# First attention of a two-layer decoder: each value product of 512 queries as two halves of 256 at neighbouring places of TensorE's order

## The reference, cut to what matters

```python
q, k, v = split(layernorm(x) @ w_qkv, 3)           # 16 heads of width 8
q1, q2 = split(q, 2); k1, k2 = split(k, 2)          # two half-heads of width 4
a1 = softmax(q1 k1^T / sqrt(8)); a2 = softmax(q2 k2^T / sqrt(8))   # 512 x 512
out = (a1 - lam * a2) @ v                           # then RMS norm per head, @ wo
```

## Time and profile before

| | |
|---|---|
| three runs | 1028.32, 1030.67, 1035.21 us; median 1030.67 |
| profiled execution | span 1028.4 us; the page gives no other time for it |
| TensorE busy (modelled ends) | 925.0 us, 90% |
| VectorE busy | 761.6 us, 74% |
| ScalarE busy | 624.5 us, 61% |
| GpSimd busy | 510.8 us, 50% |
| first value product to last | 42.9 to 393.4 us |

### The profile page before, as it was taken

How to read it: one execution, slowest core, us unless ns; L and a number is a source line. 1 busy time by engine, 2 the same in 40 slices (tenths; PEclk the granted TensorE clock), 3 DMA queues, 4 the chain that set the end, 5 groups by cost and what they waited for, 6 DMA issues and landing times. The chain is left out here.

```text
span 1028.4 us, 20270 instructions
## 1 busy us (share of the span) xinstructions
PE 925.0 (90%) x6146; PEld 480.8 (47%) x6146; DVE 761.6 (74%) x1656; ACT 624.5 (61%) x1500; POOL 510.8 (50%) x847
## 2 busy tenths in 40 slices
PE   3999999999999997899889999999999997888296
PEld 1222222222332334565455555555555564567296
DVE  7799899889999976889745666666656665676464
ACT  4388888888888883233266665665566652354164
POOL 6366666776554462100144454455445443775544
PEclk8599999999999999999999999999999997696599
DMA  4099920000000000000060000000000000000240
GB/s 103 1 237 245 245 60 1 2 1 2 2 1 0 0 1 1 1 1 1 8 206 6 15 9 7 8 13 5 8 5 13 0 2 1 0 2 16 89 122 19
DMA packets 50684, 37.49 MB, mean 36 GB/s; under 512 B 15737, under 2 KB 48677, under 8 KB 50608
## 3 DMA queue, kind: packets, MB, share of 16 engines
q1 hardware_dynamic: 48864, 32.83, 13.4%
q0 software_dynamic: 1744, 3.72, 1.1%
HBM read 15.54 MB, written 21.45 MB: 36 GB/s over the span
## 5 line engine op out<-in xcount | busy, mean ns | idle before, releaser
L725 DVE TENSOR_REDUCE a_nmax<-a_rows 128x2 f32<-128x1024 f32 x256 | 299.7, 1218 | 26.5 <-PE a_rows L439 23.6
L979 ACT ACTIVATE a_probs<-a_turned 128x512 f32<-128x512 f32 x512 | 270.0, 605 | 48.2 <-PE a_turned L465 46.9
L1451 POOL TENSOR_TENSOR a_prob<-a_prob,a_rinv 128x256 f32<-128x256 f32 (+3 forms) x128 | 159.4, 1253 | 163.9 <-DVE a_rinv L1647 163.6
L1640 DVE TENSOR_REDUCE a_nmax<-a_score 128x2 f32<-128x256 f32 (+3 forms) x128 | 105.6, 825 | 116.5 <-PE a_score L1497 112.2
L1594 ACT ACTIVATE a_prob<-a_score,a_nmax 128x128 f32<-128x128 f32 (+3 forms) x256 | 132.6, 523 | 81.9 <-DVE a_nmax L1640 81.3
L465 PE MATMUL a_turned<-a_q,a_qk 32*128 32x512 bf16 x512 | 136.9, 389 | 7.3 <-ACT a_probs L979 4.9
L424 PE MATMUL a_acc<-a_probs,a_vg 128*32 128x512 f32 x1024 | 138.1, 611 | 0.2
L439 PE MATMUL a_rows<-a_qk 32*128 32x512 bf16 x512 | 108.9, 398 | 5.9 <-DVE a_nmax L725 3.9
L465 PEld LDWEIGHTS a_turned<-a_q,a_qk 32*128 32x128 bf16 x512 | 34.9, 91 | 153.8 <-ACT a_probs L979 125.8
L1494 PE MATMUL a_score<-a_k_s,a_q_s 64*128 64x384 f32 (+3 forms) x512 | 103.7, 481 | 2.2 <-ACT a_prob L1594 1.3
L1653 DVE COPY a_pt<-a_turn 128x128 f32<-128x128 f32 (+3 forms) x224 | 92.2, 447 | 1.4 <-PE a_turn L1508 1.4
(11 more groups left out here) (351 smaller groups left out, 1580.7 us busy)
## 6 DMA issues: line engine op xcount, KB each, us to landing
xs_sorted<-a_blank SPq DMA_DIRECT2D x9, 1935.0 KB
m_m_w<-L_ffn_w SPq DMA_DIRECT2D x8, 512.0 KB, 9.2
c_xs<-xs_sorted SPq DMA_DIRECT2D x23, 129.0 KB, 2.1
g_a_wq<-L_attn_Wq SPq DMA_DIRECT2D x32, 64.0 KB, 2.1
g_X<-x SPq DMA_DIRECT2D x4, 256.0 KB, 4.7
a_wgu<-L_ffn_gate_up_proj SPq DMA_DIRECT2D x1, 1024.0 KB, 5.5
a_wdn<-L_ffn_down_proj SPq DMA_DIRECT2D x1, 512.0 KB, 6.8
g_a_wk<-L_attn_Wk SPq DMA_DIRECT2D x8, 64.0 KB, 1.9
```

Of the source, the lines that this page charges most:

```text
L725: dve.tensor_reduce(nmax[i % 2][:, p // 2, (p % 2) * 2:(p % 2) * 2 + 2], rows[n % 2][:, :, :], AX_X, ALU.max, negate=True).then_inc(row_ou ...
L979: act.activation(probs[:, (tb % 2) * 4 + j, :], turned[n % 3][:, :], ACT.Exp, scale=float(HD0) ** -0.5).then_inc(turn_out, 1)
L1451: pool.tensor_tensor(pr, pr, spread(rinv[:, t % RING, :], 2, width), ALU.mult).then_inc(scl, 1)
L1640: dve.tensor_reduce(nmax[:, t % RING, :], score[t % 2][:, :, 0:width], AX_X, ALU.max, negate=True).then_inc(mx, 1)
```

## The change

`pv_group` becomes `pv_half`. Half 0 has the group's waits and multiplies queries 0 to 255, half 1 has no wait of its own and multiplies queries 256 to 511; only half 1 counts up `pv`. Half 0 stands at the group's place k, half 1 at k + 1, so at least one `turn_tile` comes between them. Half 0 of group 0 of an even unit clears the bank's accumulation flags. In odd bodies group 2 stood at k = 15; its halves now stand at 14 and 15, so its first half comes ahead of the pair `next` 4. Products, operands and sums are otherwise the same.

```diff
-            def pv_group(i, r, tb):
-                pe.wait_ge(turn_out, turn_item(i + 1, ("exp", 4 * tb + 3)) + 1 + TURNS0 * r)
...
-                for j in range(4):
-                    last = pe.matmul(acc[32 * j:32 * j + 32, :], vg[i % 2][:, tb, j // 2, :],
-                                     probs[:, (tb % 2) * 4 + j, :], start=(tb == 0 and i % 2 == 0),
-                                     stop=(tb == SB - 1 and i % 2 == 1))
-                last.then_inc(pv, 1)
+            def pv_half(i, r, tb, half):
+                if half == 0:
+                    pe.wait_ge(turn_out, turn_item(i + 1, ("exp", 4 * tb + 3)) + 1 + TURNS0 * r)
...
+                cols = slice(half * S // 2, (half + 1) * S // 2)
                 for j in range(4):
+                    last = pe.matmul(acc[32 * j:32 * j + 32, cols], vg[i % 2][:, tb, j // 2, :],
+                                     probs[:, (tb % 2) * 4 + j, cols], start=(half == 0 and tb == 0 and i % 2 == 0),
+                                     stop=(half == 1 and tb == SB - 1 and i % 2 == 1), skip_group_check=True)
+                if half:
+                    last.then_inc(pv, 1)
...
-                    if k == 3 and has_last(i):
-                        pv_group(i - 2, r, SB - 1)
-                    if k == 6 and has_turn(i):
-                        pv_group(i - 1, r, 0)
+                    if k in (3, 4) and has_last(i):
+                        pv_half(i - 2, r, SB - 1, k - 3)
+                    if k in (6, 7) and has_turn(i):
+                        pv_half(i - 1, r, 0, k - 6)
...
-                    if k == (11, 10)[i % 2] and has_turn(i):
-                        pv_group(i - 1, r, 1)
+                    if k in (11 - i % 2, 12 - i % 2) and has_turn(i):
+                        pv_half(i - 1, r, 1, k - (11 - i % 2))
...
-                    if k == (14, 15)[i % 2] and has_turn(i):
-                        pv_group(i - 1, r, 2)
+                    if k in (14, 15) and has_turn(i):
+                        pv_half(i - 1, r, 2, k - 14)
```

More of the change, by code:

```diff
@@ L413, in _ @@
         def _(pe):
-            def pv_group(i, r, tb):
-                pe.wait_ge(turn_out, turn_item(i + 1, ("exp", 4 * tb + 3)) + 1 + TURNS0 * r)
[L417 to L422, removed]
-                for j in range(4):
-                    last = pe.matmul(acc[32 * j:32 * j + 32, :], vg[i % 2][:, tb, j // 2, :],
-                                     probs[:, (tb % 2) * 4 + j, :], start=(tb == 0 and i % 2 == 0),
-                                     stop=(tb == SB - 1 and i % 2 == 1))
-                last.then_inc(pv, 1)
+            def pv_half(i, r, tb, half):
+                if half == 0:
+                    pe.wait_ge(turn_out, turn_item(i + 1, ("exp", 4 * tb + 3)) + 1 + TURNS0 * r)
+                    if tb == 0:
+                        if i == 0:
+                            lp.ready(pe, 2)
+                        if i % 2 == 0:
+                            wait(pe, os_, i // 2 + SIX // 2 * r)
+                        pe.wait_ge(vgs, i + 1 + SIX * r)
+                cols = slice(half * S // 2, (half + 1) * S // 2)
+                for j in range(4):
+                    last = pe.matmul(acc[32 * j:32 * j + 32, cols], vg[i % 2][:, tb, j // 2, :],
[3 more added lines that the diff above has]
+                    last.then_inc(pv, 1)
             def row_pair(at, what, i, r):
```

## The result

The changed kernel takes 1051.26 us (median of four runs, 1049.08 to 1060.31), the kernel before 1030.49 (four runs, 1028.32 to 1035.21): a ratio of 1.0216, 95% interval 1.0166 to 1.0265. It is 21 us slower, where 14.4 were forecast; 1045 was predicted and the range, 1022 to 1066, holds it.

The account below looks back on a forecast made before the run. TensorE sets the pace, with VectorE close behind. A slip of 0.90 us per two bodies x 16 = 14.4 us, on 1028.4 gives 1042.8; with the profiled span 2.3 under the median, 1045 us, range 1022 to 1066.

Parts of the forecast that it names:

- Half 0.57: On TensorE, a half was taken to last 0.57 us from its first pass to the next tile.
- lead: On TensorE, 0.31 us pass from the score tile between the halves to the first pass of half 1.
- 0.14: On TensorE, two halves take 1.14 us where a group took 1.00: 0.14 us more per group.
- The walk: One odd and one even body of the first attention followed in order with fixed lags; slip 0.90 us per two bodies.
- lag of 0.71: Time after which the count of a half reaches ScalarE, 0.71 us; a whole group's took 1.13.
- Tile to its exponent 0.42.: Lag from a score tile on TensorE to its exponent on ScalarE, taken as 0.42 us.
- Group 0 starts at 329.47.: In the odd body, TensorE's group 0 was to start at 329.47 us instead of 329.30.
- The sign asked of ScalarE: If the forecast is right, ScalarE's waits behind group 0 shrink.
- ScalarE is fed: Rival: earlier tiles keep exponents in a row, saving 15 of VectorE's 23.6 us idle time, 1016 us; chance 0.12.
- No difference: Rival: a half is half a group, the 0.31 falls into buffer waits, 1032 to 1038 us; chance 0.19.
- Nothing hides: Rival, much slower: up to 3.0 us lost per two bodies, 1079 us; chance 0.11.
- That choice: Bodies with a later projection were taken to slip as much as those without, 0.90 us per two bodies.

Follow-up runs that it names:

- E1: Against the kernel before: both halves of every group directly behind each other at the group's old place; 1031.73 us, ratio 0.9985.
- E10: Changed kernel, all four groups split, plus a third block of exponents so no exponent waits for a count; 1049.69 us (one run).
- E7: Against the kernel before: only group 3 split, in even bodies alone; 1037.64 us (one run), two bodies 21.18 us.
- E12: Changed kernel, but group 3 of odd bodies has its halves directly behind each other at k = 3; 1046.03 us, ratio 1.0114.
- E5: Against the kernel before: only group 0 split, at k = 6 and 7; 1028.18 us (one profiled run), two bodies 21.00 us.
- E11: The kernel with group 0 alone split, timed over ten runs against the kernel before; 1031.04 us, ratio 0.9963.

## Why the prediction was right, and where its size was off

**The mechanism held.** Half 0.57 (0.57 taken), lead 0.32 (0.31), copy of the accumulator 1.60 us behind the group's start (329.08 - 327.49 = 1.59 walked). E1 and E10 show the cause: with nothing between the halves all of the slip goes, though the passes are as many, and with no exponent held by a count 1.19 of 1.36 stays. E1 also corrects the reading of one term: I charged 0.14 to the half; it belongs to the second change of shape. The sum is the same.

**The walk was too short.** It gave 0.90 us for two bodies; they slipped by 1.36. (By its own lag of 0.71, exponent 12 of the even body would start at 344.11 + 0.71 = 344.82, not 344.89, and the walk would end at 0.83.) Starts in us behind the first pass of group 3 in the odd body, 327.49 in the walk and 341.06 after:

| | walk | after | behind the walk |
|---|---|---|---|
| group 0 | 1.98 | 2.25 | 0.27 |
| tile 7 | 2.73 | 2.82 | 0.09 |
| group 1 | 5.03 | 5.17 | 0.14 |
| the shift's transposes | 7.58 | 7.82 | 0.24 |
| group 3, even body | 10.94 | 11.29 | 0.35 |
| group 1, even body | 15.74 | 16.21 | 0.47 |

Two terms failed.

*"Tile to its exponent 0.42."* The first exponent of each block has one more wait before it, for a count (`k % 4 == 0` in the code shown ahead), and starts 0.50 behind its tile: 350.89 to 351.39, 355.81 to 356.31. So it was before: the exponent at 344.19 stands 0.50 behind its tile:

```profile
343.69 0.38 PE L465 MATMUL a_turned<-a_q,a_qk 32*128 32x512 bf16 x1
```

The walk took 0.42 for all, and three such exponents release the buffer that TensorE waits for next: 12 in the odd body (348.23, 0.53 behind its tile at 347.70) ahead of the shift's transposes, 0 ahead of group 3, and 8 ahead of group 1 (the wait of 0.41 at 356.96). At these three places the trace falls 0.10, 0.10 and 0.09 further behind the walk. That the added wait makes the difference of 0.08 is read from these rows and was not tried.

*"Group 0 starts at 329.47."* It started 0.27 later. Group 0 of an even unit begins a new sum in `acc` and waits until ScalarE has copied the old one out (`os_`). Before, that wait was all but filled: the copy ended at 328.63 + 0.60 = 329.23 and the group started at 329.30. I moved the copy by 0.45 us and did not ask who else waits for it. But only 0.09 of the 0.27 went on: the walk already had tile 7, behind half 0, wait until 330.22 for its buffer. So the 0.45 and 0.44 us that E7 and E12 put on this one split are not what the walk missed. By its lags, without this split tile 7 would have started at 329.30 + 0.57 = 329.87, so it had charged 0.35 by then (an estimate).

The other 0.09 or so came in small steps, whose cause stays open.

**Waits.** By the walk VectorE would be idle over 10 us more; it is 18.4 (44.9 - 26.5). The sign asked of ScalarE did not come: before, no wait stood behind group 0 of the even body (eight exponents in a row from 339.59); after, there is one, 0.29 at 356.31. So the rival "ScalarE is fed" has nothing for it here, and what the prediction held against it came true: the early exponents 4 and 12 wait for half 1. "No difference" falls: the 0.31 did not vanish into waits. "Nothing hides" falls too: by the terms, eight splits cost 8 x 0.45 = 3.6 us gross, of which waits filled 2.2.

**The same slip with later projections.** Two bodies, one with such a projection, went from 21.86 to 23.13 us in most places: +1.27 against 1.36 without. That choice was good, though not everywhere: the last two of the fourteen bodies in the first stretch slipped by 0.31 (23.09 to 23.40), and its mean is 7.86 / 7 = 1.12.

**From bodies to the sum.** The last value product starts at 411.06 instead of 393.40: 17.7 us of the 20.1 by which the span grew. The other 2.4 lie behind the first attention, where nothing was changed; E1, which costs nothing, has 2.0 there (span 1030.4, last value product 393.39), so they are not the split's. Against 14.4 the first attention was 3.3 short. That it was not 16 x 0.46 = 7.4 short is in part luck: beside the smaller slip just named, the clock rose sooner in the profiled run after (granted 0.76 over 45 to 50 us, 0.50 before), and the next copy of queries and keys stood at 53.27 us, before at 54.82.

## What to carry to other kernels

Products that were cut in two cost nothing here as long as they stayed side by side; what cost was an instruction of another tile shape between them, 0.46 us of TensorE's time for a group (1.46 against 1.00). Before interleaving two shapes on the engine that sets the pace, count the changes of shape per turn of the loop. Read a lag for each kind of instruction that uses it: one that waits for one thing more was 0.08 us later here, and three of them on the path of two bodies made over half of what the walk missed. And where a step finishes later, list all who wait for it, also those whose wait is all but filled at present.

## What the runs showed of the hardware

The granted clock of TensorE moved single runs by several us. The first bodies run at the lower level (0.50), and when it rises differs from run to run, also of the same kernel: over 45 to 50 us it was 0.61 in the run of E5 and 0.50 in that of E11. Stretches of the kernel before, then of the profiled run of E12 (columns as in the earlier trace rows):

```profile
40.00:55.00 15.00, 14.23 (x77) 3.28 (x75) 10.55 (x11) 9.02 (x18) 9.30 (x20) 0.64 0.07 18
55.00:66.00 11.00, 9.94 (x80) 2.88 (x77) 9.67 (x9) 9.29 (x19) 6.23 (x18) 1.00 1.05 284
66.00:77.00 11.00, 10.82 (x83) 3.15 (x82) 10.59 (x12) 9.64 (x20) 6.44 (x19) 1.00 1.10 245
```

```profile
55.00:66.00 11.00, 10.74 (x67) 2.85 (x64) 6.32 (x7) 6.30 (x12) 4.14 (x12) 0.50 1.08 283
66.00:77.00 11.00, 11.00 (x74) 3.16 (x76) 5.63 (x6) 5.43 (x11) 2.09 (x7) 0.50 1.11 246
```

In one run the clock rises before 55 us, in the other it is still down at 77. The third copy of queries and keys behind the one at 40 us comes at 87.06 us there, in the kernel before at 76.68, and in the profiled run after at 76.41; the run took 1053.46 us where the median of its kernel is 1046.03. TensorE looks busier (11.00 of 11 us against 10.82) while doing less: VectorE's work in the stretch halves (5.63 us against 10.59). What holds the clock down was not tried.
